# Layer 1 attention: four score banks, single banks for the maxima, and later turns and read-back of sums

## What is computed

```python
q = rmsnorm(apply_rope(q, cos, sin), qn_w)        # 16 heads of 8
k = rmsnorm(apply_rope(k, cos, sin), kn_w)        # 4 heads of 8, each used by 4 query heads
scores = jnp.einsum('bthd,bshd->bhts', q, k) / np.sqrt(HD)
scores = jnp.where(causal[None, None], scores, -jnp.inf)
attn = jax.nn.softmax(scores, axis=-1)
out = jnp.einsum('bhts,bshd->bthd', attn, v)
```

## Time and profile before

| | |
|---|---|
| time, median of 3 runs | 1540.6 us (1537.18 to 1541.35) |
| span of the profiled execution | 1535.8 us, first to last instruction |
| its own time | not among the three; the median lies 4.8 us above its span |
| TensorE busy | 1313.7 us (86%) |
| VectorE busy | 976.1 us (64%) |
| ScalarE busy | 692.4 us (45%) |
| GpSimd busy | 115.2 us (7%) |
| this stage | from 1032 to 1338 us of the span |

### The profile page before, as it was taken

The page is one execution under the profiler, slowest core; times in us unless marked ns, Lnnn a source line. Parts: engine busy times, 40 slices in busy tenths (PEclk is TensorE's granted clock), DMA queues, the critical chain, the costliest instruction groups (busy, mean ns, idle before and its releaser), DMA issues. The chain is left out here.

```text
span 1535.8 us, 21410 instructions
## 1 busy us (share of the span) xinstructions
PE 1313.7 (86%) x7772; PEld 774.5 (50%) x7772; DVE 976.1 (64%) x1750; ACT 692.4 (45%) x1319; POOL 115.2 (7%) x155
## 2 busy tenths in 40 slices
PE   4688999999999999966999996526898888789998
PEld 3344444454545454444888874413343333256886
DVE  4455464545555454146999985756777666257998
ACT  2232334342424252433666665421566556525664
POOL 0000000000000000000000000120211111020000
PEclk9698999999999999987999998855899989868998
DMA  3101111120201020104576640022222210102220
GB/s 103 40 15 34 29 34 34 33 48 15 48 19 43 15 43 15 30 0 96 130 159 146 150 92 1 1 35 90 56 55 57 47 47 20 43 21 78 76 103 28
DMA packets 51476, 81.61 MB, mean 53 GB/s; under 512 B 16749, under 2 KB 34453, under 8 KB 47445
## 3 DMA queue, kind: packets, MB, share of 16 engines
q1 hardware_dynamic: 51004, 79.40, 21.1%
q10 hardware_dynamic: 384, 1.05, 0.6%
HBM read 63.75 MB, written 5.68 MB: 45 GB/s over the span
## 5 line engine op out<-in xcount | busy, mean ns | idle before, releaser
L621 DVE TENSOR_REDUCE mraw<-ps 128x1 f32<-128x512 f32 (+3 forms) x304 | 192.7, 659 | 131.1 <-PE ps L507 74.0
L1329 PE MATMUL ps<-qA 128*128 128x512 f32 x960 | 252.9, 400 | 15.2 <-POOL qA L1439 10.6
L723 ACT ACTIVATE shared<-ps 128x512 f32<-128x512 f32 (+1 forms) x216 | 119.4, 567 | 263.3 <-PE ps L540 261.9
L1046 DVE TENSOR_REDUCE mraw<-ps 128x2 f32<-128x1024 f32 (+3 forms) x160 | 173.7, 1114 | 67.6 <-PE ps L954 46.1
L1329 PEld LDWEIGHTS ps<-qA 128*128 128x128 f32 x960 | 182.1, 192 | 64.2 <-POOL qA L1439 12.3
L1101 ACT ACTIVATE shared<-ps 128x512 f32<-128x512 f32 (+2 forms) x320 | 154.4, 561 | 124.7 <-PE ps L970 124.4
L539 PE MATMUL ps<-qA,kH 128*128 128x512 f32 (+3 forms) x384 | 167.8, 447 | 5.8 <-DMA qB<-mT 5.8
L501 PE MATMUL ps<-kH,qA 128*128 128x512 f32 (+3 forms) x384 | 138.8, 415 | 34.9 <-DVE qA L611 18.8
L1393 ACT CAST qA<-shared 128x512 fp32r<-128x512 f32 x160 | 99.3, 621 | 90.4 <-DVE shared L1531 88.9
L1341 PE MATMUL ps<-qA,kH 128*128 128x512 f32 x480 | 136.3, 393 | 4.1 <-DVE qA L1455 4.1
L540 PE MATMUL ps<-qB,kL 65*128 65x512 f32 (+3 forms) x384 | 132.8, 356 | 0.0
(11 more groups left out here) (247 smaller groups left out, 1747.1 us busy)
## 6 DMA issues: line engine op xcount, KB each, us to landing
shared<-comb SPq DMA_DIRECT2D x92, 256.0 KB, 4.3
qB<-qA SPq DMA_DIRECT2D x16, 512.0 KB, 4.8
rB<-a0rec_dram SPq DMA_DIRECT2D x60, 128.0 KB, 2.9
shared<-comb SPq DMA_DIRECT2D x7, 1024.0 KB, 4.4
rB<-a1rec_dram SPq DMA_DIRECT2D x28, 128.0 KB, 2.6
e0wUp<-in_w SPq DMA_DIRECT2D x48, 64.0 KB, 4.6
qA<-q_split SPq DMA_DIRECT2D x24, 128.0 KB
q_split<-qA SPq DMA_DIRECT2D x4, 512.0 KB
```

Of the source, the lines that this page charges most:

```text
L621: nc.vector.tensor_reduce(out[:, h0:h0 + n_h, qt % 4], src, AX, ALU.max).then_inc(w_free, 1)
L723: nc.scalar.activation(probs(n)[:, hs[0]:hs[-1] + 1, lo:512], src, ACT.Exp, scale=scale)\
L1046: nc.vector.tensor_reduce(out[:, :, js[0]:js[-1] + 1, qt % 4], src, AX, ALU.max).then_inc(x_free, 1)
L1329: ins = nc.tensor.matmul(bank[0:M, :], w[par][:, at:at + M], h[:, cols], start=(r == 0), stop=(r == 2))
```

## The change

All of it is in `stage_attention8`.

1. Scores get four banks (0 to 3) instead of three. The maxima get three single banks (4 to 6) instead of two pairs.
2. A job of the maxima now covers one half i only. `MAXES` has 12 and 28 jobs instead of 6 and 14; neighbours in the list are the two halves of what was one job. A job waits until the job three before is reduced.
3. In a step TensorE's order is a fixed list: score 0, maxima, score 1, maxima, score 2, maxima, values (of two steps before), score 3, maxima. Each M takes a fourth of the step's jobs, rounded up. With 273 jobs in steps 4 to 84 a step has 3 (51 steps) or 4 (30 steps).
4. A turn comes three jobs after the last maximum of its qc, among the first maxima of the next. The fold stays right behind the last maximum, in VectorE's order. SP's waits for the turns follow.
5. `recips` moves from step 4 of a group to step 6, `normalise` from 7 to 10.
6. `pick` uses banks 4, 5 and 6, 0, and the second one also waits for all exponentials.

```diff
-    SCORE_BANKS = 3
+    SCORE_BANKS = 4
+    MAX_BANKS = 3
     O_BANK = 7
+    ORDER = "0 M 1 M 2 M V 3 M"
...
-                out += [(qt, ch, (0, 1))] if w <= 256 else [(qt, ch, (j,)) for j in range(2)]
+                out += [(qt, ch, i, js) for js in (((0, 1),) if w <= 256 else ((0,), (1,))) for i in range(2)]
...
-    GROUP_JOBS = [("max", 0, j) for j in range(len(MAXES[0]))] + [("turn", 0, 0)] + \
-                 [("max", 1, j) for j in range(len(MAXES[1]))] + [("turn", 1, 0)]
-    NJ = len(GROUP_JOBS)
-    BEFORE = len(MAXES[0]) + 1
+    DELAY0, DELAY1 = 3, 3
+    JOBS = []
+    for g in range(G):
+        some, more = ([("max", g, qc, j) for j in range(len(MAXES[qc]))] for qc in range(2))
+        last_turn = [("turn", g - 1, 1, 0)] if g else []
+        JOBS += some[:DELAY1] + last_turn + some[DELAY1:] + more[:DELAY0] + [("turn", g, 0, 0)] + more[DELAY0:]
+    JOBS.append(("turn", G - 1, 1, 0))
+    index = {job: i for i, job in enumerate(JOBS)}
+    NJ = len(JOBS) // G
+    BEFORE = index["turn", 0, 0, 0] + 1
...
-        def pair_banks(x):
-
-            return k.ps[:, (3 + 2 * (x % 2)) * 512:(5 + 2 * (x % 2)) * 512].rearrange("p (i n) -> p i n", i=2)
+        def max_bank(x):
+            return k.bank(SCORE_BANKS + x % MAX_BANKS)
+
+        def pick_bank(qc, what):
+            return k.bank((4, 5, 6, 0)[2 * qc + what])
...
-                    if idx >= 2:
-                        pe.wait_ge(x_free, idx - 1)
+                    if idx >= MAX_BANKS:
+                        pe.wait_ge(x_free, idx - MAX_BANKS + 1)
...
+                    if qc:
+                        pe.wait_ge(p_done, first_score[STEPS])
...
-                    for at in range(max(len(jobs), 1)):
-                        if at < len(jobs):
-                            score_job(n, first_score[n] + at, *jobs[at])
-                        if at % 2 == 1 or not jobs:
-                            share = -(-len(fills) // max(len(jobs) // 2 - at // 2, 1))
-                            for idx in fills[:share]:
+                    per = -(-len(fills) // max(ORDER.count("M"), 1))
+                    for token in ORDER.split():
+                        if token == "V":
+                            if n >= LAG:
+                                values(n - LAG)
+                        elif token == "M":
+                            for idx in fills[:per]:
                                 max_job(idx)
-                            fills = fills[share:]
-                    if n >= LAG:
-                        values(n - LAG)
+                            fills = fills[per:]
+                        elif int(token) < len(jobs):
+                            score_job(n, first_score[n] + int(token), *jobs[int(token)])
...
-                    nc.vector.tensor_reduce(out[:, :, js[0]:js[-1] + 1, qt % 4], src, AX, ALU.max).then_inc(x_free, 1)
+                    src = bank[:, 0:len(js) * w].rearrange("p (j w) -> p j w", w=w)
+                    nc.vector.tensor_reduce(out[:, i, js[0]:js[-1] + 1, qt % 4], src, AX, ALU.max).then_inc(x_free, 1)
+                    if n == len(MAXES[qc]) - 1:
+                        dve.wait_ge(x_free, idx + 1)
+                        if qc == 0:
+                            nc.vector.tensor_copy(k.mmax[:, 0:16], k.mraw[:, 0, 0:16]).then_inc(folded, 1)
+                        else:
+                            nc.vector.tensor_tensor(k.mmax[:, 16:32], k.mraw[:, 0, 16:32], k.mraw[:, 1, 16:32],
+                                                    ALU.max).then_inc(folded, 1)
...
-                    if n >= NU and n % NU == 4:
+                    if n >= NU and n % NU == 6:
                         recips(n // NU - 1)
-                    if n >= NU and n % NU == 7:
+                    if n >= NU and n % NU == 10:
                         normalise(n // NU - 1)
...
-                    sp.wait_ge(x_free, NJ * g + (BEFORE if qc == 0 else NJ))
+                    sp.wait_ge(x_free, index["turn", g, qc, 0] + 1)
```

More of the change, by code:

```diff
@@ L933, in max_job @@
                                             k.ident[:, :]).then_inc(x_full, 1)
                         return
-                    if j == 0:
+                    if qc == 0 and n == 0:
                         pe.wait_ge(in_ld[g % 3], landed(g))
-                    qt, ch, js = MAXES[qc][n]
+                    qt, ch, i, js = MAXES[qc][n]
                     w = keys_in(qt, ch)
                     diagonal = ch * 512 + w == (qt + 1) * P
+                    rows = row_tile(i, 64)
                     for slot, jj in enumerate(js):
[L941 to L947, removed]
+                        ins = nc.tensor.matmul(bank[:, slot * w:(slot + 1) * w],
+                                               Q[g % 3][rows, jj, qt * P:(qt + 1) * P],
+                                               kZero[g % 3][rows, ch * 512:ch * 512 + w],
+                                               start=(slot == 0), stop=not diagonal, skip_group_check=True)
@@ L948, in max_job @@
                     if diagonal:
                         n_j = len(js)
+                        ends = bank[:, 0:n_j * w].rearrange("p (j w) -> p j w", w=w)[:, :, w - P:w]
                         for part in range(2):
[L951 to L956, removed]
+                            ins = nc.tensor.matmul(ends, k.halves[rows, 0, part, :],
+                                                   k.halves[rows, 1, part:part + 1, :].broadcast_to((64, n_j, P)),
+                                                   start=False, stop=(part == 1), skip_group_check=True)
@@ L979, in pick @@
                     pe.wait_ge(x_free, NJ * G)
+                    if qc:
+                        pe.wait_ge(p_done, first_score[STEPS])
                     for what in range(2):
-                        ins = nc.tensor.matmul(k.bank(3 + 2 * qc + what)[LAST, :], k.sel8[:, what, :],
+                        ins = nc.tensor.matmul(pick_bank(qc, what)[LAST, :], k.sel8[:, what, :],
                                                oU[(G - 1) % 2][:, qc * 512:(qc + 1) * 512], start=True, stop=True)
@@ L1022, in take @@
                 def take(idx):
-                    g, j = divmod(idx, NJ)
-                    kind, qc, n = GROUP_JOBS[j]
-                    pair = pair_banks(idx)
+                    kind, g, qc, n = JOBS[idx]
+                    bank = max_bank(idx)
                     if kind == "turn":
[L1028 to L1034, removed]
                         dve.wait_ge(x_full, idx + 1)
@@ L1037, in take @@
                             dve.wait_ge(m_row[qc], 64 * g)
-                        nc.vector.tensor_scalar(k.mT[0:16, qc, :], pair[0:16, 0, 0:P], -1.0, None, ALU.mult)\
+                        nc.vector.tensor_scalar(k.mT[0:16, qc, :], bank[0:16, 0:P], -1.0, None, ALU.mult)\
                             .then_inc(x_free, 1)
```

14 lines of the change are left out of this document (6 added, 8 removed).

## The result

The changed kernel takes 1500.84 us (median of 4 runs, 1496.35 to 1503.43), the kernel before 1538.89 (4 runs, 1532.64 to 1541.35): a ratio of 0.9751, 95% interval 0.9724 to 0.9778.

What follows compares the result with a forecast made beforehand. No engine was full: a ring of short waits around an in-order TensorE. Terms of -18 + 1 + 0 - 3 = -20 us took the span from 1535.8 to 1515.8, the time to 1521 us; range 1502 to 1541.

Steps and rivals of the forecast that it cites:

- The long stretch: Steps 4 to 84: four score banks, single maxima banks and the new order shorten 218.8 us to 200; 18 us gained.
- they are part of the 18: Steps 4 to 84: TensorE's 11.0 us idle ahead of the transposes goes, counted inside the 18 us gain.
- the slots of a step: Steps 4 to 84: four matmul slots of 0.33 us plus values give 2.42 us with three maxima, 2.8 with four.
- Steps 0 to 3: First four steps: 3.5 us more VectorE work against 3.4 us of turn stalls gone; 0, bounds -4 and +4.
- The end: The last 11 steps, without maxima: score 3's wait makes 2 us, a little clock on top; 3 us gained.
- First turn: First group: the turn comes three singles later, 2.1 us less the fold's stall; 1 us lost, bounds 0 and 2.1.
- VectorE's 20 us: Steps 4 to 84: single maxima add 20 us of VectorE work, 156.5 to 176.5, covered by its idle time.
- the first rival: VectorE takes the place of the wait: stretch 213 us, a gain of 6 there, time 1533; chance 0.20.
- The signs that were named: Stretch near 200, VectorE near 176, sums' wait below 6 us; hardly any TensorE waiting at transposes or exponentials.
- The third rival: All waits vanish: VectorE near 95%, full clock in long stretch and end, 39 us gained, time 1502; chance 0.15.
- the fourth: The change shifts waits only: the reciprocal's wait grows by what the turns give back, time 1540; chance 0.04.
- The second (halves): Matmuls of opposite halves no longer pair, exposing weight loads: 25 us on top, time 1546, slower; chance 0.14.

Runs made afterwards that it cites:

- turns at once: Changed kernel with the turns put back right behind their last maximum (both delays 0): 1530.36 us, ratio 0.9958 to the kernel before.
- sums early: Changed kernel with the sums read back in step 4 and the outputs multiplied in step 7, as before: 1538.82 us, ratio 1.0021 to the kernel before.
- schedule alone: Kernel before, pairs and three score banks kept, with turns two jobs later, sums read back in step 6, outputs multiplied in step 10: 1513.01 us, ratio 0.9847.
- the kernel with later sums: Changed kernel with sums read back in step 7, outputs multiplied in step 11, the very last turn in step 85: 1498.87 us, ratio 0.9775 to the kernel before.
- halves apart: Changed kernel with the single maxima listed half by half, so wide neighbours lie in the same half of the array: 1505.74 us, ratio 0.9827 to the kernel before.

## Why the prediction missed

The stretch, split as TensorE's groups by line give it (us; "max." are the matmuls of the maxima):

| kernel | length | busy | idle: transposes | scores | max. | values | clock |
|---|---|---|---|---|---|---|---|
| before | 218.8 | 191.9 | 11.0 | 8.1 | 7.8 | 0.0 | 0.95 |
| after | 195.3 | 187.5 | 2.0 | 0.0 | 3.4 | 2.4 | 1.00 |
| turns at once | 219.9 | 199.7 | 15.8 | 0.0 | 2.0 | 2.4 | 0.91 |
| sums early | 229.5 | 201.0 | 2.0 | 0.0 | 25.2 | 1.4 | 0.90 |
| schedule alone | 202.7 | 189.3 | 1.4 | 8.6 | 3.2 | 0.1 | 0.97 |

Term by term against the stage, where 20 us were forecast and 33.0 came:

- **The long stretch, −18 forecast, −23.5 measured.** The scores' wait for a bank went as described (8.1 to nothing), and so did the transposes' (11.0 to 2.0). The step that failed is "they are part of the 18": the slots of a step were counted at an unchanged clock, scaled by the stretch before, and the 11.0 us of the turns and 3 of the sums were placed inside that result as if a step's pace set the time anyway. Turns at once and sums early show that the gain hangs on them: each alone gives back 24.6 or 34.3 us, more than the whole 18 that held banks, order and both waits. The prediction saw the clock fall behind the reciprocals and then gave it no term. In those two runs busy time rose by 12.2 and 13.5 us, at 0.09 and 0.10 less granted clock. A clock of 0.91 over 219.9 us is 2 x 0.09 x 219.9 = 39.6 us at the lower level (the first 11 of them in steps 4 to 7, ahead of the clock's rise), 0.90 over 229.5 is 45.9: 0.31 and 0.29 us for each. Steps 4 to 7 of the kernel with later sums, with the same instructions at another clock, give 0.33. Before to after, 21.9 us at the lower level go (2 x 0.05 x 218.8). At 0.33 that is an estimated 7 us, enough for the 5.5 that −18 lacks; measured is a fall of busy time by 4.4.
- **Steps 0 to 3, 0 forecast, −5.4 measured.** Both terms of the 0 were off. VectorE's extra work was put at 3.5 us; its busy time fell instead, from 29.62 to 25.00. The prediction overlooked that the steps now hold 45 singles where 24 pairs made 48, three having moved ahead of step 0 with the turn, and a copy of 3.01 us that now takes 0.17 (last section). The two turns were priced at 1.69 us each, from the long stretch; before the change TensorE waited 6.1 us at them, 4.5 of it behind the slow copy:

```profile
L932 PE MATMUL ps<-ident,mmax 128*16 128x128 f32 x2 | 0.7, 370 | 6.1 <-DVE mmax L1030 4.5 <-DVE mmax L1033 1.6
```

With 4.2 ahead of the maxima that was all of its idle time there (10.2 of 36.58; after, 0.45 of 31.16, at 0.50 in both). Turns at once leave the steps at 34.9: 3.8 us more than after, 1.7 of them ahead of the transposes, with three singles more in these steps.
- **The end, −3 forecast, −4.2 measured**, and it needs the fourth bank as said: with three it is 38.4, though at a clock of 0.72 instead of 0.89. With turns at once and with halves apart the same end runs at 1.00 and takes 29.3.
- **First turn, +1 forecast, +0.2 measured** (the lead, 14.1 to 14.3).

These differences are 5.5 + 5.4 + 1.2 + 0.8 = 12.9, all of what the stage gained beyond 20. The rest, up to the 38 of the runs, lies outside the stage.

**VectorE's 20 us** were right as a sum of durations and wrong as busy time. After, 262 reductions of 632 ns are 165.6 us; before, 131 of 1118 were 146.5, so +19.1. But reductions behind one another overlap: busy time is 150.6 as against 142.9, +7.7. In steps 0 to 3 the timeline has eight of 512 elements behind one another in 4.90 us: they start 0.60 apart, for a duration of 0.682:

```profile
1051.73 4.90 DVE L1046 TENSOR_REDUCE mraw<-ps 128x1 f32<-128x512 f32 x8
```

```profile
L1046 DVE TENSOR_REDUCE mraw<-ps 128x1 f32<-128x512 f32 x192 | 121.2, 682 | 19.8 <-PE ps L951 14.9 <-PE ps L959 4.5
```

The 0.60 was in hand, and the dearer value was taken. So the first rival, VectorE as the bound, didn't come: 83% of a stretch that is 18 us shorter than the 213 it gave.

**The signs that were named:** the stretch near 200 (195.3), transposes and exponentials holding TensorE hardly at all, the sums' wait below 6 (3.8), singles below 0.7 (0.682), and matmuls of opposite halves starting together came true. VectorE near 176 didn't (162.7). The third rival, all waits gone and a full clock (1502, at 0.15), came in its number alone: it had the stretch at 186 and the end at 24, where 195.3 and 31.1 were measured, VectorE near 95%, and nothing outside the stage. That 1500.84 lies beside it is luck. Of the fourth, sums early shows something: the wait for the sums grows to 21.1 us and the time is that of before, in part because that variant has one step less between the turn and the sums. The second (halves) is answered by halves apart: steps 8 to 84 are not longer. The Trainium skill, "TensorE: Matmul & The Clock Gate", Part 3 (Packing small matmuls), lets a weight load run beside matmuls in flight only in another row group; the earlier trace rows had not borne that out, and no run here gives a loss of the size that it would mean.

**What follows for the change.** The schedule alone is worth 20.3 of the 33.0 us of the stage and the banks with the order the other 12.7; but put into the kernel the other way round, banks and order without later turns are worth 6.7, and without later sums nothing (306.0 for the stage). The parts don't add up; each takes away what the next would be waiting for. The clock's rise is mixed into these sums too: the schedule alone has 15.30 us in steps 4 to 7, at 0.57, and in steps 8 to 84, at 1.00, it is within 2.9 us of the changed kernel.

## What to carry to other kernels

A stall of an in-order engine is priced by what runs behind it as well as by its idle time: read the granted clock of the stretch, and give a rise to full a term of its own (in these runs about a third of the time spent at the lower level). Compare two variants over steps where the clock is the same. Split a stretch into the busy and idle time of the engine that sets the pace, line by line, and take each wait out by itself before folding it into a pace per step. Work on an engine with slack is to be sized by the spacing of its instructions back to back, not by their durations.

## What had not been expected of the hardware

- The same four steps took 10.75 us with the clock at 0.96 and 14.44 at 0.58. In one variant such a late rise hid a gain of 3.0 us, in another it looked like a loss of 4.3.
- Filling a wait of TensorE with matmuls that nothing reads shortened the stretch by 6.8 us, though the fillers take 10.6 us of TensorE.
- Two single banks for the maxima instead of three cost 55 us over 81 steps, though VectorE was only 83% busy with three.
- A copy of 128x16 on VectorE took 3.01 us instead of 0.17 in the kernel before:

```profile
1074.01 3.52 POOL L1112 MEMSET qA<- 128x4096 f32 x1 [0.15 <-POOL shared L1122]
...
1074.54 3.01 DVE L1030 COPY mmax<-mraw 128x16 f32<-128x16 f32 x1
```

It started 0.53 us after GpSimd's memset and ended 0.02 after it, at 1077.55. The Trainium skill, "SBUF — State Buffer", Who interferes with whom, says that a copy in a two-port mode and a GpSimd instruction shut each other out for a whole instruction; these rows agree, though none shows which mode this copy was in. After the change the copy starts at 1066.88, ahead of the memset at 1067.83, and takes 0.17:

```profile
1066.88 0.17 DVE L1050 COPY mmax<-mraw 128x16 f32<-128x16 f32 x1
...
1067.83 3.52 POOL L1119 MEMSET qA<- 128x4096 f32 x1 [0.15 <-POOL shared L1129]
```

This is part of what shortened steps 0 to 3: the transpose behind the slow copy waited 4.46 us for it, and after the change the two transposes there wait for nothing. In the schedule alone the same copy still takes 3.01 us, but the transposes, two jobs later, wait 2.6 us in all, and these steps are at 30.6.
